# Decoder of six sublayers: stages two to six in one block, stage three unrolled and rearranged

## What is computed

```python
# 2: attention on the fixed context, 32 heads of 16
x = x + softmax(norm(x) @ ctx.T / 4 + mask) @ ctx
# 3: base product plus one of four experts of rank 8
x = x + xn @ W_up.T + lora_B[top1] @ (lora_A[top1] @ xn)     # top1 = argmax(xn @ gate_w.T + expert_bias)
# 4: powers of (gate - point) times an up product, six of them, plus silu(gate) * up, then a down product
# 5: attention of 64 features by 128 context tokens, with a skip product
```

## Time and profile before

| | us |
|---|---|
| median of three runs (lowest, highest) | 1293.69 (1292.19, 1296.74) |
| the profiled execution | 1293.84 |
| its span | 1291.9 |
| PE busy | 1138.2 |
| DVE busy | 749.5 |
| ScalarE busy | 442.6 |
| POOL busy | 399.7 |

### The profile page before, as it was taken

The page is one execution under the profiler, slowest core; times in us unless marked ns, Lnnn a source line. Parts: engine busy times, 40 slices in busy tenths (PEclk is TensorE's granted clock), DMA queues, the critical chain, the costliest instruction groups (busy, mean ns, idle before and its releaser), DMA issues.

```text
span 1291.9 us, 24210 instructions
## 1 busy us (share of the span) xinstructions
PE 1138.2 (88%) x9396; PEld 602.5 (47%) x9396; DVE 749.5 (58%) x1308; ACT 442.6 (34%) x773; POOL 399.7 (31%) x339
## 2 busy tenths in 40 slices
PE   6798986988887978898999999999978799999993
PEld 3454443666664434344344444444545444444441
DVE  6767774788886874635721531531379833646456
ACT  4565662555541113421111211211256532223230
POOL 2345485878820010009800000000043400415053
PEclk9886885999998998998999999999989999999997
DMA  6000100111101003422200000000000000000000
GB/s 219 3 3 2 28 2 27 41 39 41 36 3 40 0 10 100 137 75 75 68 1 1 1 0 0 0 1 1 1 10 9 1 1 1 17 16 32 0 33 33
DMA packets 28911, 35.73 MB, mean 28 GB/s; under 512 B 5850, under 2 KB 20467, under 8 KB 28692
## 3 DMA queue, kind: packets, MB, share of 16 engines
q1 hardware_dynamic: 27410, 34.40, 8.3%
q10 hardware_dynamic: 1410, 0.06, 0.1%
HBM read 30.10 MB, written 4.19 MB: 27 GB/s over the span
## 4 chain that ended last, share of the span: by engine, by line
PE 47%; DVE 10%; ACT 3%; issue 2%; POOL 1%; DVEq 0%; POOLq 0%; ACTq 0%
PE p_up L113 9%; PE p_up L114 8%; PE p_up L115 8%; PE p_y L113 7%; PE p_y L114 7%; PE p_y L115 7%; DVE e_den L2122 1%; ACT wd_hi L2171 1%; DVE e_top L2112 1%; PE p_up L107 1%; DVE d_xn L100 1%; DVE e_bias L2115 1%; DVE d_h_low L1848 1%; DVE d_term L1839 1%; DVE d_xt_low L156 1%
## 5 line engine op out<-in xcount | busy, mean ns | idle before, releaser
L1848 DVE TENSOR_TENSOR d_h_low<-d_hf,d_h_high 128x512 f16<-128x512 f32 (+1 forms) x40 | 32.9, 822 | 204.5 <-ACT d_h_high L1916 204.5
L113 PE MATMUL p_up<-d_xt_high,wd_hi 128*128 128x512 f16 (+1 forms) x352 | 134.4, 382 | 1.5 <-PE p_y L115 1.5
L114 PE MATMUL p_up<-d_xt_low,wd_hi 128*128 128x512 f16 (+1 forms) x352 | 134.4, 382 | 0.0
L115 PE MATMUL p_up<-d_xt_high,wd_lo 128*128 128x512 f16 (+1 forms) x352 | 134.2, 381 | 0.0
L113 PE MATMUL p_y<-wd_hi,d_h_high 128*128 128x512 f16 (+1 forms) x272 | 104.4, 384 | 8.9 <-DVE d_h_low L1848 8.9
L114 PE MATMUL p_y<-wd_lo,d_h_high 128*128 128x512 f16 (+1 forms) x272 | 104.6, 385 | 0.0
L115 PE MATMUL p_y<-wd_hi,d_h_low 128*128 128x512 f16 (+1 forms) x272 | 104.4, 384 | 0.0
L129 POOL TENSOR_SCALAR ve<-mv 128x4 f32<-128x4 f32 x8 | 2.3, 292 | 314.5 <-DVE mv L188 314.5
L165 ACT ACTIVATE d_sg<-p_up 128x512 f32<-128x512 f32 (+1 forms) x40 | 23.8, 594 | 211.8 <-PE p_up L115 211.8
L429 POOL TENSOR_TENSOR a_pt_low<-a_ex,a_pt_high 128x1024 f16<-128x1024 f32 x32 | 68.3, 2135 | 81.1 <-ACT a_pt_high L918 81.0
L2380 DVE TENSOR_TENSOR d_h_low<-d_hf,d_h_high 128x512 f16<-128x512 f32 x32 | 27.5, 859 | 71.0 <-ACT d_h_high L2469 71.0
(11 more groups left out here) (327 smaller groups left out, 2988.7 us busy)
## 6 DMA issues: line engine op xcount, KB each, us to landing
wd_raw<-in_w_d SPq DMA_DIRECT2D x16, 616.0 KB, 3.7
wd_raw<-in_w_f SPq DMA_DIRECT2D x8, 578.0 KB, 3.7
X<-in_x SPq DMA_DIRECT2D x4, 1024.0 KB, 12.3
wd_lo<-in_ctx_t SPq DMA_DIRECT2D x128, 32.0 KB
out_x<-wd_raw SPq DMA_DIRECT2D x16, 256.0 KB, 2.0
wd_lo<-in_ctx SPq DMA_DIRECT2D x32, 64.0 KB, 2.4
wd_raw<-in_w_c SPq DMA_DIRECT2D x1, 1096.0 KB, 12.5
wd_hi<-in_Wo SPq DMA_DIRECT2D x1, 1024.0 KB
```

Of the source, the lines that this page charges most:

```text
L113: nc.tensor.matmul(ps, st[0], mv[0], start=start, stop=False)
L114: nc.tensor.matmul(ps, st[0], mv[1], start=False, stop=False)
L115: return nc.tensor.matmul(ps, st[1], mv[0], start=False, stop=stop)
L1848: nc.vector.tensor_tensor(hid[1][0:n, d % NH, :], value, hid[0][0:n, d % NH, :], ALU.subtract).then_inc(h_ready, 1)
```

## The change

Stages two to six share one block (`stages_bcdef`); no engine waits for all the others between them, and the lists of `part_b`, `part_c`, `part_d`, ... stand one behind the other on each engine. PSUM is shared by them (`p_up`, `p_y`, four banks each), and so are the buffers of `share_buffers`; stage three's weights and `lora` now lie in the last columns of `wd_hi`, and stage two's probabilities in `wf_hi` and `wf_lo`, so that pieces 0 to 2 of stage four's weights can be made early.

Stage three is unrolled over sixteen tiles. Its norms are made by ScalarE, as `rstd * x - mean * rstd`; POOL makes rstd and `nmr` chunk by chunk in stage two (`rstd_next`). The gate has five operations. z is split in high and low (`zcat`: high, high, low, 96 values), and so is lora (high, low, high, 96 rows), so that the turn of z and `delta` are one fp16 product each. `delta` now stands ahead of the products of the next tile. Tiles 0 and 1 are normalized, transposed and halved in the last units of stage two; chunk 0 of stage four likewise in the last tiles of stage three. ScalarE makes the high half of weight pieces 0 to 2 in iterations 3, 7 and 11 and scales the raw piece in place, and POOL subtracts. In stage four the small work for stage five moves on PE and ScalarE.

The core of the diff (the new `part_c` in full but for buffers, the hooks in stages two and four, what moves in stage four):

```diff
 def part_b(nc, held, a, es):
...
+                def rstd_next(c):
+                    tiles = slice(TC * c, TC * c + TC)
+                    pool.wait_ge(stats, TC * c + TC)
+                    pool.wait_ge(vb_ready, VB * (min(TC * c + 2 * TC, NT) + 2))
+                    rstd_steps(nc, pool, held, tiles, held.rs_c + 2 * c)
+                    pool.wait_ge(held.rs_ready, held.rs_c + 2 * c + 2)
+                    nc.gpsimd.tensor_tensor(held.nmr[:, tiles], held.mv[:, tiles, 0], held.rstd[:, tiles, 0],
+                                            ALU.mult).then_inc(held.nmr_ready, 1)
+                    pool.wait_ge(held.nmr_ready, 2 * c + 1)
+                    nc.gpsimd.tensor_scalar(held.nmr[:, tiles], held.nmr[:, tiles], -1.0, None,
+                                            ALU.mult).then_inc(held.nmr_ready, 1)
+                for c in range(1, NC):
                     for i in range(TC):
                         tile(c, i, True)
+                    rstd_next(c - 1)
+                rstd_next(NC - 1)
...
                 for n in range(-2, N + 2):
+                    if n == N + 1:
+                        p.c.low(v, 0)
+                        p.c.low(v, 1)
                     if n >= 2:
                         norm_o(n - 2)
...
                 for n in range(-2, N):
+                    if n in (N - 4, N - 2):
+                        p.c.norm(act, (n - N + 4) // 2)
                     if 0 <= n + 1 < N:
                         expo(n + 1)
...
+                    if n == N:
+                        p.c.trans(pe, 0)
+                        p.c.trans(pe, 1)
                     if n >= 1:
                         attend(n - 1)
...
+def part_c(nc, held, a, es):
...
+    def gpsimd(pool, weights):
+        for c in range(NC):
+            if c < 3:
+                weights(c)
+            rstd_chunk(nc, pool, held, c, stats, held.rs_d + 2 * c)
...
+    def gate(v, t):
+        k = 4 * t
+        v.wait_ge(aux_ready, t + 1)
+        nc.vector.scalar_tensor_tensor(logit[:], p_aux(t)[:, 0:EX4], 1.0 / (XS * WS), held.ebias[:],
+                                       ALU.mult, ALU.add).then_inc(gated, 1)
+        v.wait_ge(gated, k + 1)
+        nc.vector.tensor_reduce(top[:, 0:1], logit[:], AX.X, ALU.max).then_inc(gated, 1)
+        v.wait_ge(gated, k + 2)
+        nc.vector.scalar_tensor_tensor(pick[:], logit[:], top[:, 0:1], held.rank[:],
+                                       ALU.is_equal, ALU.mult).then_inc(gated, 1)
+        v.wait_ge(gated, k + 3)
+        nc.vector.tensor_reduce(top[:, 1:2], pick[:], AX.X, ALU.max).then_inc(gated, 1)
+        v.wait_ge(gated, k + 4)
+        nc.vector.scalar_tensor_tensor(
+            z32[:], pick[:].rearrange("p (e b) -> p e b", b=1).broadcast_to([128, EX4, R8]), top[:, 1:2],
+            p_aux(t)[:, EX4:CG].rearrange("p (e r) -> p e r", e=EX4), ALU.is_equal, ALU.mult).then_inc(zp_ready, 1)
+
+    def low_z(v, t):
+        v.wait_ge(zh_ready, t + 1)
+        nc.vector.scalar_tensor_tensor(zcat[:, t % 2, 2 * RZ:3 * RZ], z32[:].rearrange("p e r -> p (e r)"),
+                                       ZS / (XS * WS), zcat[:, t % 2, 0:RZ], ALU.mult, ALU.subtract).then_inc(zl_ready, 1)
...
+    def vector(v, norm_next, low_next):
+        rows = slice(RZ, 2 * RZ)
+        v.wait_ge(lora_hi, 1)
+        nc.vector.scalar_tensor_tensor(held.lora[rows, :], held.lora_raw[rows, :], BS, held.lora[rows, :],
+                                       ALU.mult, ALU.subtract).then_inc(lora_lo, 1)
+        for t in range(NT):
+            if t:
+                update(v, t - 1)
+            gate(v, t)
+            if 1 <= t < NT - 1:
+                low(v, t + 1)
+            low_z(v, t)
+            if t == NT - 2:
+                norm_next(0)
+                norm_next(1)
+            if t:
+                measure(v, t - 1)
+        low_next(0)
+        norm_next(2)
+        low_next(1)
+        norm_next(3)
+        update(v, NT - 1)
+        low_next(2)
+        low_next(3)
+        measure(v, NT - 1)
+
+    def norm(act, t):
+        act.wait_ge(held.nmr_ready, 2 * (t // TC) + 2)
+        if t >= 2:
+            act.wait_ge(t_ready, t - 1)
+        nc.scalar.activation(xn[:, t % 2, :], held.X[:, t, :], ACT.Identity, bias=held.nmr[:, t:t + 1],
+                             scale=held.rstd[:, t, 0:1]).then_inc(xn_ready, 1)
...
+    def scalar(act, weights, high_next):
+        high(act, 0)
+        high(act, 1)
+        nc.scalar.activation(ident_h[:], held.ident[:], ACT.Copy).then_inc(ident_ready, 1)
+        nc.scalar.activation(held.lora[0:3 * RZ, :], held.lora_raw[0:3 * RZ, :], ACT.Copy, scale=BS).then_inc(lora_hi, 1)
+        norm(act, 2)
+        high_z(act, 0)
+        for t in range(1, NT):
+            copy_z(act, t - 1)
+            if t + 1 < NT:
+                high(act, t + 1)
+            else:
+                high_next(0)
+            high_z(act, t)
+            if t + 2 < NT:
+                norm(act, t + 2)
+            if t % 4 == 3 and t < 12:
+                weights(t // 4)
+        high_next(1)
+        copy_z(act, NT - 1)
+        for i in range(2, TC):
+            high_next(i)
...
+    def turn_z(pe, t):
+        if t == 0:
+            pe.wait_ge(ident_ready, 1)
+        pe.wait_ge(zl_ready, t + 1)
+        if t:
+            pe.wait_ge(zc_ready, t)
+        nc.tensor.matmul(p_zt[0:3 * RZ, :], zcat[:, t % 2, :], ident_h[:], start=True, stop=True).then_inc(zt_ready, 1)
+
+    def delta(pe, t):
+        if t == 0:
+            pe.wait_ge(lora_lo, 1)
+        pe.wait_ge(zc_ready, t + 1)
+        nc.tensor.matmul(p_out(t), zt[:, t % 2, :], held.lora[0:3 * RZ, :], start=False, stop=True).then_inc(out_ready, 1)
+
+    def tensor(pe, turn_next):
+        products(pe, 0)
+        for t in range(1, NT):
+            turn_z(pe, t - 1)
+            if t + 1 < NT:
+                trans(pe, t + 1)
+            else:
+                turn_next(0)
+            delta(pe, t - 1)
+            products(pe, t)
+        turn_next(1)
+        turn_z(pe, NT - 1)
+        turn_next(2)
+        delta(pe, NT - 1)
+        turn_next(3)
...
 def part_d(nc, held, a, es, c_part):
...
+            def low_first(pool, q):
+                part = slice(PD * q, PD * q + PD)
+                if q == 0:
+                    pool.wait_ge(*held.b_done)
+                pool.wait_ge(wd_scaled, q + 1)
+                nc.gpsimd.tensor_tensor(held.wd_lo[:, part], raw[:, q % 2, :], held.wd_hi[:, part],
+                                        ALU.subtract).then_inc(wd_split, 1)
+
+            def high_first(act, q):
+                part = slice(PD * q, PD * q + PD)
+                act.wait_ge(wd_in[q % 2], 16 * (q // 2) + 16)
+                nc.scalar.activation(held.wd_hi[:, part], raw[:, q % 2, :], ACT.Copy, scale=WS).then_inc(wd_high, 1)
+                act.wait_ge(wd_high, q + 1)
+                nc.scalar.activation(raw[:, q % 2, :], raw[:, q % 2, :], ACT.Copy, scale=WS).then_inc(wd_scaled, 1)
...
-                                nc.vector.tensor_tensor(kept[:], before, keep[:], ALU.mult).then_inc(keep_ready, 1)
+                                nc.vector.tensor_tensor(keep[:], before, keep[:], ALU.mult).then_inc(keep_ready, 1)
...
-                        if weights and d in (0, 1):
-                            for t in ((0, 1) if d == 0 else (2,)):
+                        if weights and d == 0:
+                            e.fold_in(act)
+                        if weights and d in (1, 2):
+                            for t in ((0, 1) if d == 1 else (2,)):
                                 e.keys_in(act, t)
...
-                    if fresh:
-                        e.fold(pe)
                     for j in range(3):
                         up(c, j, fresh)
-                        if fresh:
-                            e.make_keys(pe, j)
+                        if fresh and j == 0:
+                            pe.wait_ge(c_part.updated, NT)
+                            e.fold(pe)
+                        if fresh and j == 1:
+                            e.make_keys(pe, 0)
+                            e.make_keys(pe, 1)
+                        if fresh and j == 2:
+                            e.make_keys(pe, 2)
```

437 lines of the change are left out of this document (188 added, 249 removed).

## The result

| | before | after |
|---|---|---|
| median of the interleaved runs, us | 1293.66 (4 runs, 1292.19 to 1296.74) | 1260.52 (4 runs, 1253.88 to 1264.73) |
| profiled execution / its span, us | 1293.84 / 1291.9 | 1253.88 / 1252.2 |

The ratio is 0.9736, with a 95% interval of 0.9689 to 0.9783: 33.1 us less by the medians, 39.7 by the two spans. The changed kernel scatters over 11 us, and the profiled execution was the quickest of the four.

What follows compares the result with a forecast made beforehand. PE's own instructions were taken to bound stage three, with holes at either side. Terms -7.8 - 12.7 + 6.2 + 1.2 + 0.5 - 12.0 - 4.7 - 1.2 = -30.5 took 1293.8 to 1263 us, range 1252 to 1279.

Steps and rivals of the forecast that it cites:

- Into stage three, -7.8: From stage two's end to stage three's first turn of z: 401.76 becomes 394.0, -7.8 us, bounds -9.5 to -6.
- PE's tile, 3.9: Stage three: PE's tile falls from 4.75 to 3.9 us, fifteen times, -12.7 us, bounds -15 to -7.
- rival B: Stage three: DVE's ring sets the pace, 0.45 more per tile, 6.8 us more, total 1270; chance 0.13.
- Three pieces, +6.2: Stage three, iterations 3, 7 and 11: ScalarE's weight piece stalls PE 2.05 us, three times, +6.2; bounds 1.5 and 3 each.
- POOL, +1.2: Stage three: POOL's subtraction of each weight piece holds DVE, 0.4 left over per piece, +1.2 us; bounds 0 and 9.
- rival A: Stage three: PE's clock falls at all four new stalls, 7.6 + 1.2 us more, total 1272; chance 0.15.
- POOL's rstd: Stage two: four small rstd blocks on POOL hold DVE somewhat, +0.5 us.
- To stage four, -12.0: Stage three's last product to stage four's first up product: 17.4 us becomes 5.4, DVE longest, -12.0; bounds 4.5 and 7.
- Stage four's first chunk, -4.7 and -1.2: Stall of 3.08 us and its low clock go, -4.7; half of up product's slow start, -1.2; bounds 0 and -7.5.
- D: Stage three: chip holds PE at 1.2 GHz, 3.6 us more per tile, slower than before, 1303; chance 0.04.
- E: Stage boundaries: norms or turns still wait for DVE in the old order, 10 and 4 us stay, 1277; chance 0.04.
- C: Smaller stalls (2.7), POOL holds nobody (1.2), up product at full clock (1.2), DVE early into stage three (2): 1256; chance 0.09.

Runs made afterwards that it cites:

- The run without stage two's hook: Changed kernel with stage three's tiles 0 and 1 normalized, transposed and halved only behind stage two's last statistics: 1263.25 us, ratio 0.9792.
- the run without pieces: Changed kernel with weight pieces 0 to 2 moved from stage three back to stage four's start, on ScalarE and DVE: 1254.8 us, ratio 0.9712.
- the repeat: Changed kernel traced again with the same code, nothing altered: span 1259.8 us, 32.1 less than before.
- fourteen: All 14 runs of the changed kernel, its code unaltered: median 1257.8 us.

## Why the prediction was right, point by point

**Into stage three, -7.8: measured -8.1.** The order of events was as traced; the five gate operations took 1.09 us and the turn of z came 4.9 us behind stage two's last product instead of 5.3. The run without stage two's hook gives back 4.4.

**PE's tile, 3.9: measured 3.70.** This is the term whose size was furthest off. I gave 0.6 to turn, transposes and a rest of the wait, and 2.7 + 0.4 + 0.2 to the products; starts on PE give 0.59, and 2.58 + 0.31 + 0.22, and there was no wait. The 2.7 and 0.4 were distances between starts in the tile of the earlier trace rows, and each held a seam of about 0.1 us that the new tile doesn't have. Two more lines of that tile:

```profile
416.88 0.18 PE L115 MATMUL c_p_aux<-wc_hi,c_xt_low 128*128 128x36 f16 x1
...
419.39 0.38 PE L115 MATMUL c_p_out<-wc_hi,c_xt_low 128*128 128x512 f16 x1
```

The first base product starts 0.13 us behind the last gate product (416.88 to 417.01), where gate products stand 0.025 apart, and the branch in fp32 starts 0.31 behind the last base product (419.39 to 419.70), where base products stand 0.215 apart. The second seam is there in all fifteen tiles and went with the fp32 branch; the first is there in a few tiles only, of which this was one. With the floor of 55.7 us that the run without pieces shows, the term is -15.5 instead of -12.7. The ring of DVE and ScalarE that I feared as an equal bound (rival B) is slower than PE only with the norm on DVE: 3.94. No run puts the fp32 branch or the old gate back; that the fp16 branch brings most of this rests on the timelines (1.12 us and its seam against 0.22).

**Three pieces, +6.2, and POOL, +1.2: measured +9.2.** The two terms themselves were close: the stall was 1.89, not 2.05, and the wait for POOL in the first piece's interval 0.42, where 0.4 were forecast; the first two intervals with a piece took 2.6 and 2.5 us more, where the terms give 2.45. What the sum lacked was the rest: 1.2 us by the clock that fell behind the third stall, which I had only in rival A, and 0.2 in the tile behind each of the other two. The tile's error and this one have opposite signs, 2.8 and 1.8 us: that stage three as a whole came within 1.0 of its forecast is in part luck. ScalarE's norm took 0.80 us, not the 0.68 of a step with one operand per partition. The Trainium skill, page "ScalarE: Activation LUTs", section "What ACT_TABLE_LOAD costs", gives a price for an operation and for each such operand, from which one estimates 799 ns for 512 columns with two; the trace agrees, with 798 ns as the median of 13.

**POOL beside DVE.** The mechanism was as I read it from the earlier trace rows, and how much lies beneath other work was the question: 0.42 us of waiting where the stall had gone before, 1.16 where it stands alone. DVE's update and the gate's first operation, which read one tensor from PSUM and one from SBUF, ran at their 0.69 and 0.15 beside the same POOL step. The Trainium skill, page "SBUF — State Buffer", section "SBUF: two separate sides", says that VectorE's operations in a two-port mode or with two inputs in SBUF compete with a GpSimd operation that reads SBUF for a shared pair of ports, and that the loser waits for the whole instruction. By that rule, the trace agrees on both sides: held and not held. The run with the low halves on DVE confirms that it is POOL. In stage two POOL's rstd held nothing that can be seen, 177.4 us against 177.4 (0.5 was forecast).

**To stage four, -12.0: measured -12.4**, with DVE as the longest list, as traced: PE waits 1.19 us for its norm and 1.41 for its low half. No run undoes this part, so how the 12.4 divide between the block's end, rstd and the early tiles isn't shown.

**Stage four's first chunk, -4.7 and -1.2: measured -7.3 at the down product after it.** The stall of 3.08 and the low clock behind it went as forecast, and with them a stall of 0.27 that wasn't in the sum. The up product ran at full clock from the start, which I had given half. That was luck: it did so in 9 of the 12 traces of new kernels whose pieces are ready in time, and not in the other 3. Undoing the order costs 5.0 without that clock and 6.7 with it. Of this 7.3, the stretch to the end kept 4.5 in the repeat and 7.5 in the profiled execution; the difference lies in the clock of later stages, which the change leaves alone.

**The rivals.** A came true in one of three stalls: 1.2 us instead of 7.6. The Trainium skill, page "TensorE: Matmul & The Clock Gate", section "HAM oscillation — how this bites in real kernels", tells of repeated waits that each let the clock fall; no row here shows that for stalls of 1.89 us as a rule: one in three did it. B is refuted by DVE's 0.39 us of waiting per tile, D by clocks of 1.00 in the plain tiles (0.96 and 0.98 in the one behind the third stall, in the repeats), E by the boundaries. C was right in the up product (1.2) and wrong in the stalls and POOL; of DVE's earliness 0.3 us came of its 2. The errors were -2.8 (tile), +1.8 (pieces and POOL), -1.4 (first chunk, at the down product), -0.3 and -0.4 (boundaries) and -0.5 (stage two): -3.6 in all, part of which later stages took back, and the forecast of 1263 stands 2.5 us above the median of the four runs and 5 above that of fourteen.
